# A four-layer graph network on one core: layer 0's coefficients from its feature product, smaller norm factors, and a new step order

## What is computed

```python
# layer 0: attention whose scores pair up neighbouring nodes
h  = x @ others_weight;  u1 = h @ a1;  u2 = h @ a2
e  = u1[:, idx1] + u2[:, idx2]          # idx1, idx2: (2m, 2m+1), taken // n or % n
e  = where(e >= 0, e, 0.1 * e)
out = softmax(where(adj > 0, e, NEG), axis=1) @ h + x @ self_weight
# layer 1: attention, norm, then a GIN layer with an MLP
s   = leaky(s_src[:, :, None] + s_dst[:, None, :])
g   = relu(layernorm((softmax(masked s) * A) @ (x @ Wp + bp)) * gat_g + gat_b)
z   = relu(layernorm(((1 + eps) * g + A @ g) @ W1 + b1) * mlp_g + mlp_b)
out = relu(z @ W2 + b2 + g)
# layer 2: attention as in layer 1, out = elu(attention @ (x @ W) + bias)
# layer 3: two products, one for the diagonal of a softmaxed edge matrix, one for the rest
out = diag(A) @ (x @ W[0]) + offdiag(A) @ (x @ W[1]) + bias
```

## Time and profile before

| | us |
|---|---|
| median of 3 runs | 1011.76 (1009.36 to 1011.84) |
| the profiled execution, its own time | 1009.46 |
| its span, first to last instruction | 1007.7 |
| PE busy, idle | 943.0, 64.7 |
| mean granted TensorE clock | 0.979 of full |

### The profile page before, as it was taken

How to read it: one execution, slowest core, us unless ns; L and a number is a source line. 1 busy time by engine, 2 the same in 40 slices (tenths; PEclk the granted TensorE clock), 3 DMA queues, 4 the chain that set the end, 5 groups by cost and what they waited for, 6 DMA issues and landing times. The chain is left out here.

```text
span 1007.7 us, 21096 instructions
## 1 busy us (share of the span) xinstructions
PE 943.0 (94%) x7355; PEld 901.4 (89%) x7355; DVE 866.1 (86%) x2526; ACT 632.5 (63%) x1655; POOL 566.6 (56%) x1171
## 2 busy tenths in 40 slices
PE   5879999999999989999989999999999999997998
PEld 4779998998988989998989999899999998997897
DVE  6879898899979999978989987789989887887973
ACT  3435746875777755676675756777458676666751
POOL 3416356655477662763748645736646475556750
PEclk9978999999999999999999999999999999999999
DMA  5011000000011010011000101100100100000012
GB/s 136 1 36 28 2 1 1 2 1 1 2 43 42 2 44 1 1 43 43 2 1 2 43 2 43 43 1 13 32 1 2 42 2 1 17 7 2 1 43 63
DMA packets 38069, 19.97 MB, mean 20 GB/s; under 512 B 3142, under 2 KB 37452, under 8 KB 37964
## 3 DMA queue, kind: packets, MB, share of 16 engines
q1 hardware_dynamic: 36080, 18.42, 6.6%
q10 hardware_dynamic: 1884, 0.21, 0.2%
HBM read 10.23 MB, written 8.39 MB: 18 GB/s over the span
## 5 line engine op out<-in xcount | busy, mean ns | idle before, releaser
L450 ACT ACTIVATE Y<-X,SM 128x128 f32<-128x128 f32 x512 | 204.3, 489 | 70.8 <-POOL SM L446 70.6
L687 PE MATMUL ps<-HE,PT 128*128 128x129 f32 x2048 | 240.2, 276 | 2.7 <-ACT HE L999 1.7
L687 PEld LDWEIGHTS ps<-HE,PT 128*128 128x128 f32 x2048 | 233.5, 192 | 4.1 <-ACT HE L999 1.9
L1311 DVE SCALAR_TENSOR_TENSOR PT<-ps,CE,maskT 128x512 f32<-128x512 f32 x256 | 173.0, 741 | 13.3 <-PE ps L811 13.0
L442 POOL TENSOR_TENSOR SM<-SM,minus_half 128x8 f32<-128x8 f32 x96 | 162.9, 1696 | 7.6
L431 POOL TENSOR_TENSOR SM<-ST 128x8 f32<-128x8 f32 x96 | 29.7, 310 | 230.8 <-DVE ST L1176 230.8
L687 PE MATMUL ps<-W,HT 128*128 128x128 f32 (+1 forms) x768 | 125.9, 312 | 0.0
L687 PEld LDWEIGHTS ps<-W,HT 128*128 128x128 f32 x768 | 116.4, 194 | 8.8
L1176 DVE BATCH_NORM_STATS2 ST<-X 128x6 f32<-128x128 f32 x512 | 104.7, 277 | 2.6 <-DMA X<-in_x_dram 1.0
L704 PE MATMUL ps<-ident,Y 128*128 128x128 f32 x640 | 86.3, 282 | 13.2 <-ACT Y L450 11.0
L704 PEld LDWEIGHTS ps<-ident,Y 128*128 128x128 f32 x640 | 74.5, 146 | 16.8 <-ACT Y L450 14.1
(11 more groups left out here) (260 smaller groups left out, 2355.5 us busy)
## 6 DMA issues: line engine op xcount, KB each, us to landing
X<-in_x_dram SPq DMA_DIRECT2D x32, 256.0 KB, 3.5
out_dram<-X SPq DMA_DIRECT2D x32, 256.0 KB, 2.8
adj_raw<-in_adj_dram SPq DMA_DIRECT2D x4, 256.0 KB, 3.8
W<-in_L_gnn_W_dram SPq DMA_DIRECT2D x2, 64.0 KB, 3.8
W<-in_L_gnn_W_dram SPq DMA_DIRECT2D x1, 128.0 KB, 3.5
bias<-in_L_gnn_bias_dram SPq DMA_DIRECT2D x2, 64.0 KB, 3.9
Wo<-L_gnn_others_weight_dram ACTq DMA_DIRECT2D x1, 64.0 KB, 3.2
feat1w<-in_L_gnn_Wp_dram ACTq DMA_DIRECT2D x1, 64.0 KB, 3.6
```

The costliest lines, as they stand in the source:

```text
L450: a = nc.scalar.activation(dst[:, n, 0:F], src[:, n, 0:F], func, scale=SM[s][:, S_RSTD, n:n + 1], bias=SM[s][:, S_SHIFT, n:n + 1])
L687: return nc.tensor.matmul(o, w, m, start=start, stop=stop, skip_group_check=True)
L1311: a = V.scalar_tensor_tensor(out=PT[r][:, j, :], in0=o, scalar=CE[s][:, c:c + 1], in1=maskT[:, j, :].bitcast(F32), op0=ALU.max, op1=ALU.mult)
```

## The change

1. `feat0` moves ahead of `coef0`, has the two attention vectors as columns 128 and 129 of its weights (`feat0w`), opens 3 banks with 3, 3 and 2 tiles, and is read at once by ACT into `HE`. A new DVE step `ucol0` takes these two columns, keeps even or odd rows by a mask (`parity`) and splits them for fp32r; `coef0` on PE is then 2 fp32r products with `halve`, which brings rows 2m and 2m+1 to row m. `split0` on DVE works from `HE` in 2 products.
2. The factor of every norm is left halved (L445 goes); the reads that follow use scale 2.0, and `gat_g` and `mlp_g` are doubled once. The attention norm adds eps times the squared sum to the variance instead of multiplying with inverse sums.
3. `norow` holds 1/N, and ACT writes the mean of empty rows in 4 reads; POOL's product goes.
4. In gin1 the rest of the diagonal block stands beside two blocks of `gin_hi` in one operand of 384 columns (`gin_mix`), and the high product has the other 256.
5. `TURNS` and `HOMES` are new. In PE's new order 0.feat0 follows 0.norm0, and between 0.coefb0 and 0.agg0 stands 1.cmax0; between feat0 and coef0 of a group there stands at least one step, of the groups 9 and e one each: 5.feat2, a.att2a.

```diff
     ("norm0", 2, "pe act"),
+    ("feat0", 3, "pe act"),
+    ("ucol0", 0, "dve"),
     ("coef0", 1, "pe dve"),
     ("cmax0", 1, "pe dve act"),
-    ("feat0", 2, "pe"),
...
+        MIX = [(0, P), (0, 2 * P), (2, 0), (2, P)]
...
         def rstd_of(pool, link, s, inv):
...
+            if inv:
+                TT(sm[:, S_INV, :], Y[s][:, :, F], Y[s][:, :, F], ALU.mult)
...
+            if inv:
+                TS(sm[:, S_INV, :], sm[:, S_INV, :], 4.0 * LN_EPS, TINY * 1e-7, ALU.mult, ALU.max)
...
             if inv:
-                link(TT(sm[:, S_VAR, :], sm[:, S_VAR, :], sm[:, S_INV, :], ALU.mult))
-                link(TT(sm[:, S_VAR, :], sm[:, S_VAR, :], sm[:, S_INV, :], ALU.mult))
-                link(TS(sm[:, S_VAR, :], sm[:, S_VAR, :], 4.0 * LN_EPS, None, ALU.add))
+                link(TT(sm[:, S_VAR, :], sm[:, S_VAR, :], sm[:, S_INV, :], ALU.add))
             link(TT(sm[:, S_RSTD, :], sm[:, S_VAR, :], minus_half[:], ALU.pow))
-            if inv:
-                link(TT(sm[:, S_RSTD, :], sm[:, S_RSTD, :], sm[:, S_INV, :], ALU.mult))
-            link(TS(sm[:, S_RSTD, :], sm[:, S_RSTD, :], 2.0, None, ALU.mult))
...
+                link(nc.gpsimd.memset(evens[:], 0.0))
+                link(nc.gpsimd.affine_select(out=stairs[:], in_=work1[:, 0:2, 0:P], compare_op=ALU.is_ge, fill=0.0, base=0,
+                                             pattern=[[P, 2], [-2, P]], channel_multiplier=1))
+                nc.gpsimd.affine_select(out=halve[:], in_=stairs[:], compare_op=ALU.is_ge, fill=0.0, base=1,
+                                        pattern=[[-P, 2], [2, P]], channel_multiplier=-1)
+                nc.gpsimd.affine_select(out=evens[:], in_=evens[:], compare_op=ALU.not_equal, fill=1.0, base=0,
+                                        pattern=[[-2, P // 2]], channel_multiplier=1).then_inc(made["evens"], 1)
+                pool.wait_ge(made["maskT"], 2)
+                for j in range(T):
+                    lo, c = MIX[j]
+                    nc.gpsimd.tensor_copy(gin_mix[:, j, P - lo * P // 2:3 * P - lo * P // 2], maskT[:, j, c:c + 2 * P].bitcast(F32))
...
+                nc.gpsimd.tensor_scalar(gat_g[:], gat_g[:], 2.0, None, ALU.mult)
+                nc.gpsimd.tensor_scalar(mlp_g[:], mlp_g[:], 2.0, None, ALU.mult)
...
                 def coef0(u, s):
-                    for b in range(G):
-                        turned(u, "norm0", s, b)
+                    pe.wait_ge(sig["ucols"][s], count(u.g, 1, 0))
                     o, done = open_tile(u, "coef0", s, 0)
-                    for t in range(HALF):
-                        for odd in range(2):
-                            for b in range(G):
-                                c = 4 * ((t * 2 + odd) * G + b)
-                                r0 = t * 2 * P + odd
-                                mm = MM(o[:, c:c + 4], HT[s][:, b, r0:r0 + 2 * P - 1:2], wcols0[:], True, True)
+                    cols = UC[s][:].rearrange("p t c l -> p t (c l)")
+                    for h in range(2):
+                        mm = MM(o[:, 0:4 * TG].rearrange("p (t c) -> p t c", t=HALF), halve[:, h, :], cols[:, h::2, :],
+                                h == 0, h == 1)
...
                 def feat0(u, s):
+                    for b in range(G):
+                        turned(u, "norm0", s, b)
+                    for n in range(3):
+                        o, done = open_tile(u, "feat0", s, n)
+                        for c, r in enumerate(range(3 * n, min(3 * n + 3, TG))):
+                            mm = MM(o[:, c * WD:(c + 1) * WD], blk(s, r % G, r // G), feat0w[:], True, True)
                         mm.then_inc(done, 1)
...
+                def whole(ap, j):
+                    if j in (0, T - 1):
+                        return ap.rearrange("p (k c) -> p k c", c=P)[:, 0::T - 1, :]
+                    return ap[:, (j - 1) * 2 * P:j * 2 * P]
                 def gin1(u, s):
...
-                            for m in (LO, HI):
-                                MM(o, m[s][:, j * G + b, :], gin_hi[:, j, :], j == 0 and m is LO, False)
-                            mm = MM(o[:, j * P:(j + 1) * P], HI[s][:, j * G + b, :], gin_lo[:, j, :], False, j == T - 1)
+                            lo, c = MIX[j]
+                            hi = HI[s][:, j * G + b, :]
+                            MM(o, LO[s][:, j * G + b, :], gin_hi[:, j, :], j == 0, False)
+                            MM(whole(o, j), hi, whole(gin_hi[:, j, :], j), False, False)
+                            first = min(c, j * P)
+                            mm = MM(o[:, first:first + 3 * P], hi, gin_mix[:, j, :], False, j == T - 1)
...
+                def feat0(u, s):
+                    rows = HE[s][:].rearrange("p r c -> p (r c)")
+                    for n in range(3):
+                        o, read = filled(u, "feat0", s, n)
+                        first, last = 3 * n * WD, min(3 * n + 3, TG) * WD
+                        A(rows[:, first:last], o[:, 0:last - first], ACT.Copy).then_inc(read, 1)
...
                 def sums2(u, s):
                     o, read = filled(u, "sums2", s)
-                    A(SR[s][:], o[:, 0:G * P].rearrange("p (b f) -> p b f", b=G), ACT.Copy,
-                      scale=1.0 / N).then_inc(read, 1)
+                    m = HT[s][:].rearrange("p b n -> p (b n)").rearrange("p (t r) -> p t r", t=T)
+                    for t in range(T):
+                        a = A(m[:, t, :], o[:, 0:G * F], ACT.Identity, scale=norow[:, t:t + 1])
+                    a.then_inc(read, 1)
...
-                    link(TT(m, repeat(SR[s][:].rearrange("p b f -> p (b f)"), T), bcast(norow[:], G * F), ALU.mult))
...
-                        link(V.tensor_scalar(SM[s][:, S_INV, :], sums, TINY, None, ALU.max))
-                        V.reciprocal(SM[s][:, S_INV, :], SM[s][:, S_INV, :])
...
+                def ucol0(u, s):
+                    for n in range(3):
+                        read_by_act(u, "feat0", s, n)
+                    src = HE[s][:, :, F:F + 2].rearrange("p (t b) c -> p t b c", b=G)
+                    both = US[s][:].rearrange("p t (o b c) -> p t o b c", o=2, b=G)
+                    for odd in range(2):
+                        a = V.tensor_scalar(both[:, :, odd], src, parity[:, odd:odd + 1], None, ALU.mult)
+                    link(a)
+                    link(V.tensor_copy(UC[s][:, :, :, 0], US[s][:]))
+                    V.tensor_tensor(UC[s][:, :, :, 1], US[s][:], UC[s][:, :, :, 0].bitcast(F32),
+                                    ALU.subtract).then_inc(sig["ucols"][s], 1)
...
                 def split0(u, s):
-                    for h in range(2):
-                        o, read = filled(u, "feat0", s, h)
-                        v, r = o.rearrange("p (r f) -> p r f", f=F), slice(4 * h, 4 * h + 4)
-                        a = V.tensor_tensor(YF[s][:, r, :], v, bcast(SM[s][:, S_A, r], F), ALU.mult)
-                    a.then_inc(sig["scaled"][s], 1)
...
+                    V.tensor_tensor(YF[s], VA[s], bcast(SM[s][:, S_A, :], F), ALU.mult).then_inc(sig["scaled"][s], 1)
+                    V.tensor_tensor(VA[s], VA[s], bcast(SM[s][:, S_B, :], F), ALU.mult).then_inc(sig["scaled"][s], 1)
```

More of the change, by code:

```diff
@@ L293, in gnn_kernel @@
         sig = {n: [sem(f"{n}_{s}") for s in range(NS)] for n in (
-            "stored", "var", "rstd", "normed", "extent", "scaled", "hi", "lo", "range", "dexp", "by_act",
+            "stored", "ucols", "var", "rstd", "normed", "extent", "scaled", "hi", "lo", "range", "dexp", "by_act",
             "by_pool", "gated")}
@@ L297, in gnn_kernel @@
         x_loaded = [sem(f"x_loaded_{s}") for s in range(NS)]
-        Y, LOW, HE, LOWB, HT, HI, ST, US, CD, CF, CE, CS, MX, SM, DS, HS, SR = ([] for _ in range(17))
+        Y, LOW, HE, LOWB, HT, HI, ST, US, UC, CD, CF, CE, CS, MX, SM, DS, HS = ([] for _ in range(17))
         def slot_first(s):
@@ L322, in slot @@
             HS.append(sb(f"HS{s}", [P, G, 2]))
-            SR.append(sb(f"SR{s}", [P, G, F]))
         for s in range(NS // 2):
@@ L383, in gnn_kernel @@
             m_loc = sb("m_loc", [P, MB], F32, sc)
-            diagv = sb("diagv", [P, T, P], F32, sc)
+            diagv = below[:, :, 0:P]
             rmax = sb("rmax", [P, T], F32, sc)
@@ L956, in turn_rows @@
                         elif name == "norm2":
-                            a = A(HT[s][:, b, :], o, ACT.Relu, accum_out=HS[s][:, b, 0:1])
+                            a = A(HT[s][:, b, :], o, ACT.Relu, scale=2.0, accum_out=HS[s][:, b, 0:1])
                         else:
-                            a = A(HT[s][:, b, :], o, ACT.Relu)
+                            a = A(HT[s][:, b, :], o, ACT.Relu, scale=2.0)
                         a.then_inc(read, 1)
@@ L972, in split0 @@
                 def split0(u, s):
-                    act.wait_ge(sig["scaled"][s], count(u.g, 1, 0))
+                    act.wait_ge(sig["scaled"][s], count(u.g, 2, 0))
                     A(HI[s][:], YF[s], ACT.Copy).then_inc(sig["hi"][s], 1)
```

(10 more changed lines are left out.)

116 lines of the change are left out of this document (57 added, 59 removed).

## The result

The changed kernel takes 965.67 us (median of 4 runs, 962.44 to 966.11) against 1011.8 us for the one before (1009.36 to 1012.96): a ratio of 0.954, with a 95% interval of 0.9513 to 0.9567. That is 46 us less, where 30 were forecast; it lies in the range, at the place that the prediction had kept for the order doing more. The profile of after is of its fastest execution (962.44 us, span 960.5), that of the control of one of 966.61 us.

The account below looks back on a forecast made before the run. The prediction took PE to bound the kernel, DVE close behind. PE work -30.7, waits -2, POOL hold-ups +1 and DVE density +2 gave -29.7 us, so 980 us, range 962 to 1001.

Parts of the forecast that it names:

- the order doing more: Rival: freed banks and the early stretch give 8 to 15 us more, 965 to 972 us; chance 0.17.
- coef0 on PE: Two fp32r products replace 8 in each of 16 groups, 0.30 us for 1.81: -24.2 us.
- gin1 on PE: Columns regrouped as 512, 256 and 384 remove a weight-load wait, 0.055 us in each of 128 turns: -7.0 us.
- feat0 on PE: Its eight fp32 products grow from 128 to 130 columns: +0.5 us of PE work.
- DVE: DVE's work: split0 gains nothing, attention's sums save 10 us, ucol0 adds 10 to 20; ends at 866 to 876 us.
- POOL: Norm chains 0.31 us shorter, doubling and mean product gone; PE waited 7 times for scaled rows: -2 us of waits.
- split0 blocking POOL: A third of split0's 32 new SBUF products hold up POOL operations: 12 us on POOL, +1 us of time.
- its rival at 1014: Rival: all 35 us of blocked POOL operations delay scales that PE waits for, 1014 us; chance 0.02.
- The order: The new order of all steps and new banks: 0 us, with bounds of -8 to +8.
- DVE density: In the densest stretches, cut by 3%, DVE would need 96 to 97% busy: +2 us.
- the DVE rival at 995: Rival: DVE takes over, its idle time shrinking by only half of what is needed, 995 us; chance 0.15.
- The new chain: Rival: layer 0's coef0 waits for feat0, ACT's reads and ucol0, up to 7.4 us a group: 1050, mildly 1027; chance 0.05.

Follow-up runs that it names:

- the control: The changed kernel itself, unaltered, timed a second time on another chip: 966.0 us, ratio 0.9556 to the kernel before.
- the old costs: Changed kernel with coef0's 8 old products added unused, gin1's old form, the factor's doubling and attention's inverse sums put back: 1021.5 us, ratio 1.0091.
- fills: Changed kernel with products that nobody reads issued in two early waits of PE, 963.0 us, or in five, 962.8 us.
- the two halves of the norm edits: Changed kernel with only the factor's doubling put back on POOL in 96 norms, 978.1 us, or only attention's inverse sums, 972.0 us.

## Why the prediction was right in most, and where it was wrong

- **coef0 on PE**, -24.2: right, a little low. Where PE waits for nothing the step costs 0.22 us, not 0.30; the 0.08 for an fp32r product behind fp32 work did not show. 16 x (1.81 - 0.22) = 25.4.
- **gin1 on PE**, -7.0: right, or a little high. 0.53 us a turn; undoing it cost 4.7 (6.6 by the ratios), doing it in the old order gave 6.0. The extra 0.05 us went in all turns when no product of 128 columns stood ahead any more, as the prediction's reading wants it; that it was the weight load is still its reading.
- **feat0 on PE**, +0.5: its work did not grow (33.2 us, 34.1 in the earlier trace rows), but 6.0 us of waits stand ahead of it, 5.6 of them for rows turned just before. The prediction followed the chain from feat0 on and never asked what feat0 itself would wait for when it was moved forward. These waits stand in the first groups only.
- **PE busy** "near 912", idle 65: 901 and 59 (903.6 and 61 in the control). The work accounts for 25.4 + 6.7 + 0.9 = 33.0 of the 41.8. The granted clock can account for the rest: by an estimate, 1 - 0.979 of 1007.7 is 21.2 us lost and 1 - 0.989 of 960.5 is 10.6, so 10.6 fewer, some of them in PE's waits.
- **DVE** at 866 to 876: wrong, 840.7. ucol0 is right (12.7 in 10 to 20), split0 too; the hold-ups behind POOL's operations were overlooked. Nothing shows that they touched the time.
- **ACT** +40: right, 37.2.
- **POOL**, "PE waited 7 times for scaled rows, so -2": this is the step that failed. The norm edits, with the two DVE operations that go with them, measured 23 us in the new order. In the old order the term would have been off by little (4.6 with the mean's edit). The sum took the slack of the old order's chains and the work of the new one; but the order had been changed with the costs, and with it (and with layer 0's new form) the chains' slack: 4.6 us became 23, with PE's work light or full. Count what may lie on the way to the end, here by the estimate some 28 to 38 of 96 chains, not what PE happened to wait for in the old trace. That the total still came into the range is in part luck: the terms that the runs give are 29 for PE's work and 23 for the norms, less some 8 for what the new order and layer 0's new form cost by themselves (11.3 less 3.5).
- **split0 blocking POOL**, 12 us of POOL and +1 of time, and its rival at 1014: it happened, in 8 operations and 7 us, so the rival is out and the third of the products that the prediction took was too much. Its cost in time was not measured. With the rest of the order changed POOL was held up less than before in sum (38 us against 60), but not everywhere: the first operation of a norm's chain takes 257 ns against 310, the last one 292 against 271.
- **The order**, 0: near its bound of +8 as far as it can be told (with the old costs it is 2 to 9 us slower than before, layer 0's new form included), wrong as a separate term. The likely mechanism that I named for more, freed banks and the early stretch, holds only for the second: the early stretch gave part of the head's 7.7 us (4.0 in the control), and fills give 2 to 3 of the control's time. Freed banks were not tried alone.
- **DVE density**, +2, and the DVE rival at 995: no sign of either. DVE worked 94.1 of 100 us beside PE's 96.2, and PE's waits for the maximum stayed at 2.6 us.
- **The new chain**, 1050 or 1027: 0.5 us of waits for ucol0. The price of 7.4 us a group assumed the worst of ACT and DVE each time; the groups have a step between.

What stays open: the new coef0 in the old order was not tried, since it needs other places for its steps and banks, so whether the old order would have given all of its 25 us isn't known, nor whether it is the order or layer 0's new form that makes the norm chains count. The mean's edit was not tried alone. The 5.4 us by which 60.9 is more than 55.5, and the 5 that the two halves of the norm edits leave, have no cause shown.

## What to carry to other kernels

A change that comes with a new order can't be priced by the waits of the old one: take the length of each shortened chain times the number of such chains, and keep that as the far end of the range. An order written for one set of costs may be no better than the old one with another: with the old costs this one was slower. And look at the median and the maximum beside the mean of a group: where the mean is well above the median, look the long ones up in the timeline. Here they stood beside an operation of the other engine.

## What the runs showed of the hardware

- A DVE operation on 4 elements that mostly takes 0.22 us took up to 2.42, and one of 1.22 us took 2.94, beside a POOL operation on two 128x1024 operands in SBUF. After, with another order, neither was longer than 0.23 and 1.23. It goes the other way too: a POOL operation of 0.20 us took 2.45 beside two DVE products of two SBUF operands.
- A first fp32r product of 32 columns behind fp32 products costs no more than the second: 0.11 us each where PE waits for nothing. The earlier trace rows had shown 0.20 for a first one of 256 columns.
- Two executions of one program differed by 4.2 us; 3.7 of them arose where the control's PE work ran at 1.2 GHz and the other's at 2.4 (granted 0.81 and 0.90 from 50 to 100 us). The middle behind it took the same time to 0.1 us. Products that nobody reads, in the waits there, came with a grant of 0.97 to 1.00 and a median 3 us lower (2 by the ratios).
